# A two-layer gated cross-attention and expert model on one core: one pair's softmax sums moved from GpSimd's fold to ones products, and the first expert slots turned earlier

## What is computed

```python
x = x + tanh(g_xattn[0]) * L0_xattn(layernorm(x), ctx_1024, ...)    # 16 heads of 8
x = x + tanh(g_ffn[0])   * L0_ffn(layernorm(x), ...)                # 8 experts with low-rank parts, top 2
x = x + tanh(g_xattn[1]) * L1_xattn(ctx_1024, layernorm(x), ...)    # 16 heads of 64
x = x + tanh(g_ffn[1])   * L1_ffn(layernorm(x), ...)                # 8 experts, top 1
```

```python
dots = einsum('bhid,bhjd->bhij', q, k) * scale      # 256 queries, 768 keys (512 context, 256 latents)
attn = softmax(dots, axis=-1)
out  = einsum('bhij,bhjd->bhid', attn, v)           # then all heads @ Wout
```

## Time and profile before

| | |
|---|---|
| runs, us | 718.05 (717.65 to 720.27), n = 3 |
| profiled execution, us | 715.89 |
| its span, us | 714.1 |
| mean granted TensorE clock | 0.978 |
| TensorE, VectorE, ScalarE, GpSimd busy, us | 654.0, 526.4, 374.0, 354.2 |

### The profile page before, as it was taken

The page is one execution under the profiler, slowest core; times in us unless marked ns, Lnnn a source line. Parts: engine busy times, 40 slices in busy tenths (PEclk is TensorE's granted clock), DMA queues, the critical chain, the costliest instruction groups (busy, mean ns, idle before and its releaser), DMA issues.

```text
span 714.1 us, 14356 instructions
## 1 busy us (share of the span) xinstructions
PE 654.0 (92%) x5392; PEld 491.8 (69%) x5392; DVE 526.4 (74%) x1074; ACT 374.0 (52%) x581; POOL 354.2 (50%) x450
## 2 busy tenths in 40 slices
PE   5779999999989889899999999999999999779994
PEld 4656666666778777676777767777677776557884
DVE  5767887776598887798677777778889778746533
ACT  3656776665543444554464455545554446416652
POOL 3294444450034422566667566765666566680131
PEclk9779999999999999999999999999999999999997
DMA  8200000000300003000001000002000002010211
GB/s 187 25 0 2 2 2 3 2 2 1 120 3 1 0 1 111 2 1 1 2 1 31 16 2 16 17 14 61 1 3 1 1 2 60 21 51 12 67 49 56
DMA packets 35268, 16.97 MB, mean 24 GB/s; under 512 B 12824, under 2 KB 33648, under 8 KB 35072
## 3 DMA queue, kind: packets, MB, share of 16 engines
q1 hardware_dynamic: 33680, 14.94, 8.0%
q0 software_dynamic: 512, 1.05, 0.5%
q10 hardware_dynamic: 1008, 0.07, 0.1%
HBM read 12.05 MB, written 3.93 MB: 22 GB/s over the span
## 4 chain that ended last, share of the span: by engine, by line
PE 67%; DVE 20%; issue 6%; POOL 2%; ACT 1%; DMA 1%; SPq 0%; POOLq 0%; DVEq 0%; ACTq 0%
PE ps L1938 64%; DVE o L1638 3%; DVE pmax L1625 2%; PE ps L1949 2%; DVE mx L1308 2%; DVE kql L1613 1%; DVE exm L1504 1%; DVE pmax L1622 1%; POOL y_tok L726 1%; POOL xs_scratch L718 1%; PE ps L2042 1%; DMA raw<-in_L_xattn_Wproj_dram 1%; PE ps L2587 1%; DVE wsel L1501 0%; DVE rt_y L1415 0%
## 5 line engine op out<-in xcount | busy, mean ns | idle before, releaser
L1015 ACT ACTIVATE p<-ps 128x1024 f32<-128x1024 f32 x96 | 96.5, 1025 | 151.2 <-PE ps L1938 151.2
L752 POOL TENSOR_TENSOR acc<-p 128x256 f32<-128x256 f32 x128 | 94.9, 773 | 74.3 <-ACT p L1015 74.2
L1938 PE MATMUL ps<-p,v 128*64 128x256 f32 (+1 forms) x1280 | 123.4, 384 | 0.8 <-DVE xr L1334 0.6
L1938 PE MATMUL ps<-kqh 64*128 64x256 f32 (+1 forms) x640 | 111.3, 374 | 13.6 <-DVE pmax L1622 4.0
L758 POOL TENSOR_TENSOR acc<-acc,p 128x256 f32<-128x256 f32 x128 | 91.8, 749 | 54.2 <-ACT p L1015 54.1
L1622 DVE TENSOR_REDUCE pmax<-ps 128x2 f32<-128x1024 f32 x64 | 78.2, 1222 | 33.5 <-PE ps L1938 33.4
L1308 DVE TENSOR_REDUCE mx<-ps 128x1 bf16<-128x512 f32 x128 | 82.5, 687 | 26.6 <-PE ps L1938 26.0
L1938 PEld LDWEIGHTS ps<-p,v 128*64 128x64 f32 (+1 forms) x1280 | 66.1, 126 | 46.8 <-issue 15.3
L1938 PEld LDWEIGHTS ps<-kqh 64*128 64x128 f32 x640 | 62.6, 193 | 43.1 <-issue 34.4
L655 POOL TENSOR_SCALAR q<-qst,rmask 128x256 fp32r<-128x256 f32 x64 | 58.8, 939 | 59.2 <-ACT qst L775 59.2
L879 ACT ACTIVATE p<-ps 128x1024 f32<-128x1024 f32 x64 | 65.5, 1025 | 23.1 <-PE ps L1938 21.5
(11 more groups left out here) (318 smaller groups left out, 1431.5 us busy)
## 6 DMA issues: line engine op xcount, KB each, us to landing
w_raw<-in_L_ffn_W_dram SPq DMA_DIRECT2D x8, 256.0 KB, 2.7
ys_scratch<-y SPq DMA_DIRECT2D x22, 64.0 KB, 1.5
ctx_all<-in_ctx_dram SPq DMA_DIRECT2D x4, 256.0 KB, 5.6
raw_kv<-in_L_xattn_Wkv_dram SPq DMA_DIRECT2D x1, 1024.0 KB, 4.9
ctx_all<-in_L_ffn_W_dram SPq DMA_DIRECT2D x4, 256.0 KB, 3.6
w_raw_late<-in_L_ffn_W_dram SPq DMA_DIRECT2D x4, 256.0 KB, 3.8
xs_scratch<-xnA SPq DMA_DIRECT2D x1, 832.0 KB, 4.5
xs_rawA<-xs_scratch SPq DMA_DIRECT2D x3, 256.0 KB, 3.2
```

The costliest lines, as they stand in the source:

```text
L752: ins = pool.tensor_tensor(acc1[:, at], p1[:, s, 0, at], p1[:, s, 1, at], ALU.add)
L1015: act.activation(p1[:, g % 2, u, :], bank(2 * (n % 2), 2), ACT.Exp, scale=SCALE1).then_inc(a_exp1.sem, 1)
L1938: return pe.matmul(o, lhsT, rhs, start=start, stop=stop)
```

## The change

It makes three edits.

1. `UNFOLDED = G1 - 2 = 30`. GpSimd leaves out the adds and the fold of pair 30 (its scatters stay where they are), and the counts of g_acc and g_fold are made to fit. `sums1(30)` no longer waits for a fold: it multiplies each of the six chunks of p by the ones, both heads, 12 calls that accumulate into the same half of bank 6.
2. On TensorE `slots_turn(0)` is moved ahead of `outputs1_pairs(B - 1, range(NPAIR - 1))`.
3. On VectorE `slots_low(0)` is moved to between `w2_low(4)` and `w2_low(5)`; before it stood behind `w2_low(7)`.

```diff
--- before.py
+++ after.py
@@ -282,6 +282,7 @@
         TURN_SLOTS = (1, 5, 9, 11, 14, 18)
         EXP_SLOT = 4
         RANK_AT = (bank(7)[:, NQ:NQ + (TOKEN_TILES[0] + 1) * E], bank(7)[:, 0:(TOKEN_TILES[1] + 1) * E])
+        UNFOLDED = G1 - 2
         onecol = ident[:, MAXROW:MAXROW + 1]
         TURN_BANK = [4] + [7] * (B - 1)
         ROUTE_BANK = [5] + [7] * (B - 1)
@@ -744,20 +745,23 @@
                 s = g % 2
                 if g == G1 - 2:
                     scattered(0, xnA, range(TOKEN_TILES[0]))
+                if g == UNFOLDED:
+                    continue
+                n = g - int(g > UNFOLDED)
                 pool.wait_ge(a_exp1.sem, a_exp1.after(g, 2))
-                if g >= 1:
-                    pool.wait_ge(g_fold.sem, g)
+                if n >= 1:
+                    pool.wait_ge(g_fold.sem, n)
                 for c in range(4):
                     at = slice(c * NQ, (c + 1) * NQ)
                     ins = pool.tensor_tensor(acc1[:, at], p1[:, s, 0, at], p1[:, s, 1, at], ALU.add)
                 ins.then_inc(g_acc.sem, 1)
                 pool.wait_ge(a_exp1.sem, a_exp1.after(g, 3))
-                pool.wait_ge(g_acc.sem, g_acc.after(g, 1))
+                pool.wait_ge(g_acc.sem, g_acc.after(n, 1))
                 for c in range(4):
                     at = slice(c * NQ, (c + 1) * NQ)
                     ins = pool.tensor_tensor(acc1[:, at], acc1[:, at], p1[:, s, 2, at], ALU.add)
                 ins.then_inc(g_acc.sem, 1)
-                pool.wait_ge(g_acc.sem, g_acc.after(g, 2))
+                pool.wait_ge(g_acc.sem, g_acc.after(n, 2))
                 if g >= 2:
                     pool.wait_ge(e_den1.sem, g - 1)
                 a = acc1[:, :].rearrange("p (j n q) -> p j n q", j=2, n=2)
@@ -1114,7 +1118,7 @@
             def gelu(tile):
                 act.wait_ge(e_up.sem, tile + 1)
                 if tile == 0:
-                    act.wait_ge(g_acc.sem, g_acc.after(G1, 0))
+                    act.wait_ge(g_acc.sem, g_acc.after(G1 - 1, 0))
                 if tile >= 2:
                     act.wait_ge(e_hidT.sem, tile - 1)
                 act.activation(hid1[:, tile % 2, :], bank(UP_BANK[tile % 2]), ACT.Gelu).then_inc(a_gelu.sem, 1)
@@ -1766,7 +1770,7 @@
             def hidden_low(tile):
                 dve.wait_ge(a_hidH.sem, tile + 1)
                 if tile == 0:
-                    dve.wait_ge(g_acc.sem, g_acc.after(G1, 0))
+                    dve.wait_ge(g_acc.sem, g_acc.after(G1 - 1, 0))
                 if tile >= 2:
                     dve.wait_ge(e_down.sem, tile - 1)
                 dve.tensor_tensor(hidT_l[:, tile % 2, :], bank(HID_BANK[tile % 2]), hidT_h[:, tile % 2, :],
@@ -1894,9 +1898,11 @@
                 if g in W2_PAIRS:
                     w2_low(W2_PAIRS.index(g))
                 if g == G1 - 1:
-                    for e in range(2, E):
+                    for e in range(2, 5):
                         w2_low(e)
-            slots_low(0)
+                    slots_low(0)
+                    for e in range(5, E):
+                        w2_low(e)
             divide1(G1 - 1)
             for tile in range(SLOTS_ALL):
                 if tile == EXP_SLOT:
@@ -2448,9 +2454,16 @@
                 ins.then_inc(e_pv1.sem, 1)
 
             def sums1(g):
-                pe.wait_ge(g_fold.sem, g + 1)
-                for j in range(2):
-                    ins = mm(bank(6)[j * D1:(j + 1) * D1, NQ:2 * NQ], onesf[:, :], fold1[:, g % 2, j, :])
+                o = [bank(6)[j * D1:(j + 1) * D1, NQ:2 * NQ] for j in range(2)]
+                if g == UNFOLDED:
+                    for k in range(TK):
+                        for j in range(2):
+                            ins = mm(o[j], onesf[:, :], p1[:, g % 2, k // 2, j * BANK + (k % 2) * NQ:j * BANK + (k % 2 + 1) * NQ],
+                                     k == 0, k == TK - 1)
+                else:
+                    pe.wait_ge(g_fold.sem, g + int(g < UNFOLDED))
+                    for j in range(2):
+                        ins = mm(o[j], onesf[:, :], fold1[:, g % 2, j, :])
                 ins.then_inc(e_den1.sem, 1)
 
             def outputs1(b):
@@ -2657,8 +2670,8 @@
 
             expert = list(experts_in(0))
             pe.wait_ge(d_route.sem, d_route.after(0, 5))
+            slots_turn(0)
             outputs1_pairs(B - 1, range(NPAIR - 1))
-            slots_turn(0)
             sums1(G1 - 1)
             up1(0)
             for tile in range(SLOTS_ALL):
```

## The result

The changed kernel takes 712.28 us in the median of 12 runs (709.87 to 714.83). The kernel before is at 716.83 us in 12 runs (713.61 to 720.27), of which the prediction knew three, with a median of 718.05. The medians differ by 4.55 us. The ratio is 0.9934, 95% interval 0.9915 to 0.9952: by it 4.7 us less, between 3.4 and 6.1. The profiled execution takes 712.78 us with a span of 710.8, against 715.89 and 714.1: 3.3 us of span.

The account below looks back on a forecast made before the run. The seam's chain was taken to run through GpSimd's late fold of pair 30 and VectorE's reciprocal, leaving TensorE a 3.72 us hole. Gains of 2.2 and 1.4 us sum to 3.6: 718.05 - 3.6 = 714.4 us, range 712.4 to 716.5.

Parts of the forecast that it names:

- link 1: Pair 30's sums: 24 ones entries in 2.64 us replace GpSimd's adds and fold, freeing pair 31's p x v 2.2 us earlier.
- (C): Rival: pair 30's ones products cost double, 5.3 us, so gain 0.95 us, 717.1 us; chance 0.08.
- Links 2 to 4: Pair 31's scores, a 1.4 us TensorE gap at the upper clock, p x v from 632.97, slots_turn(0) at 635.71, xs_l wait gone.
- (B): Rival: the new TensorE gap of 1.4 us lowers the clock for 3.4 us; gain 1.9 us, 716.1 us; chance 0.10.
- Links 5 and 6: Pair 31's fold is ready before its sums need it, so no wait; up1(0) starts at 639.85 instead of 643.47.
- Link 7: Moved w2_low(5..7) delay pair 31's divide; last output products wait 0 to 1.1 us, 0.6 covered by VectorE's later chain.
- the last sum: Whole-kernel forecast: base 718.05 us, the median of the runs shown, less the 3.6 us seam gain, 714.4 us.
- rival (A): Low clock stretch from 621.49, ahead of pair 30's p x v, is absent; gain 5.2 us, 712.8 us; chance 0.22.

Follow-up runs that it names:

- e5: Changed kernel with the 12 ones products of pair 30 done twice: 715.20 us, ratio 0.9970.
- b1: Kernel before, no edit, traced again: 28.0 us from slot_u to up1(0).
- e1: Changed kernel with only the sums of pair 30 by ones products, slots_turn(0) and slots_low(0) back in their old places: 713.64 us, ratio 0.9953.
- e9: Changed kernel with pair 30's ones products ahead of its p x v (bank 7) and 14 small useless products in TensorE's idle piece: 710.03 us, ratio 0.9917.
- e3: Changed kernel with 14 small useless products in TensorE's idle piece ahead of pair 31's last maxima: 711.12 us, ratio 0.9918.
- b2: Kernel before, no edit, traced again: 29.3 us from slot_u to up1(0).
- e8: Kernel before with 54 small useless products in the hole ahead of pair 30's ones product: 715.99 us, ratio 1.0003.
- e10: Kernel before with 14 small useless products in the earlier idle piece and 84 in the hole: 715.28 us, ratio 0.9990.
- e0: Changed kernel as it stands, timed again: 712.39 us, ratio 0.9936.
- e7: Changed kernel with slots_low(0) back behind w2_low(7), slots_turn(0) still early: 713.37 us, ratio 0.9952.

## Why the forecast was right in its links and short in its size

**Removed wait (link 1): right.** 24 entries, 2.76 us for 2.64 + 0.17 forecast, no idleness before them, reciprocal at 630.87 for 630.70. The entries did not take 0.2 us each, so (C) is out: e5 shows 0.22 us for a whole product. The output products, with a weight of 128x128 and a moving slice of 128 columns, cost as much with half the columns: 28 entries in 3.23 us are 0.23 us for each of the 14. So the products with a 128x64 weight cost half of that for a column. The starts differ too: in the trace of the changed kernel two entries of the ones products start 0.006 us apart (628.064 and 628.070), the next two 0.21 us later (628.279 and 628.285), and each is recorded with 0.38 us, while in the trace of before the output entries start one by one, 0.11 us apart (638.138, 638.249, 638.361). What makes the entries go in pairs is not shown; no run changed the form of these products.

**Links 2 to 4: right.** Gap 1.16 us for 1.4, p x v at 633.14 for 632.97, slots_turn at 635.89 for 635.71. The granted clock stayed at 1.00 over the new gap (1.16 us in each) in all four traces of the changed kernel; (B) is out as far as they go.

**Links 5 and 6: right.** Fold not waited for, up1(0) at 640.18 for 639.85; from slot_u the gain is 27.4 - 24.0 = 3.4 us for 3.6. The moves alone are 1.0 to 1.2 us of it for my 1.4.

**Link 7: right, one sign missed.** 0.67 us of waiting for the divide, forecast 0 to 1.1, free up to 0.6. That is just over the 0.6 that I had named as a sign of being wrong, and the wait for xnB, which I said would stay, is gone. Both are the cover of link (7) at work: this wait takes the place of that one, and the part behind up1(0) is no longer than before.

**The step that failed** is the last sum: "the median of the runs shown lies 2.2 above the profiled run, and the same difference from it gives 718.05 - 3.6". It comes out 2.1 us over the 712.28 measured, and both of its terms are mis-sized.
- The base, 1.2 us. I took the median of three runs for the kernel's: 718.05, where twelve give 716.83. The three lie in the upper part of a spread of 713.6 to 720.3; that is chance, not a mechanism. With 716.83 my gain would have given 713.2, inside the range.
- The gain, 3.6 us for 4.55 by the medians. Between the two traces it is 3.4, so the links were priced right. What I had wrong is one trace's clock taken for the kernel's, on both sides of the change.
  - Before the change I took the 1.12 us of the four fold entries and one low stretch behind the hole as given. The trace that I had shows the cheapest of four: 27.4, 28.0, 28.7, 29.3 us, mean 28.4. The others cost up to 1.9 us more, and no case of mine had them.
  - After the change I kept the early low stretch and gave rival (A), without it, a chance of 0.22. It is absent in two of four traces (24.0 and 24.0 with it, 22.4 and 22.4 without, mean 23.2).

By the four traces on each side the seam gains 28.4 - 23.2 = 5.1 us, with a standard error of 0.6. Over the timed runs of the study the means are 716.6 us (100 runs of before) and 712.2 (23 of the changed kernel), 4.4 us with a standard error of 0.4. The two agree within their errors, and 4.4 is the better figure. Both errors went the same way; and my range ended at 712.4 with the centre of case (A) at 712.8, so it left a spread of 0.4 us below a case that turned out to be half of the traces.

**Open.** What decides which low stretches an execution gets is not shown. Nor was the part ahead of slot_u taken apart, 614.5 to 618.1 us. It goes together with the clock at the start: in the first 60 us the granted clock is 0.50 for 13.7 us in eight of the eighteen traces (0.89 in the mean) and for 17.1 in ten (0.86). Seven of the eight have slot_u at 614.5 to 615.1, and all of the ten have it at 615.8 or later. Three traces lie another 2 us later (b1, e1, e9) for a reason that wasn't looked for. The slowest runs of the changed kernel (714.6 to 714.9) have no trace; they may have e5's longer early stretch, 6.8 us, or those 2 us.

## What to carry to other kernels

The hole in TensorE's work cost its waiting and the clock behind it, and the second part differed from run to run (3.4 to 7.3 us at 0.50 in four traces of one kernel); before pricing such a hole's removal, trace several executions and take the mean, and don't take the median of three runs for the base when single runs spread by 6 us. And when a wait is removed, ask what it had been hiding: here the stretch at 0.50 ahead of the hole, free before, became 1.5 us of the path in two of four traces, and with fourteen products without use in an idle piece (0.95 us in e3) it was absent from all four traces taken.

## What the hardware showed that I had not expected

- TensorE's granted clock was 0.50 for 10.2 us in one piece (b2, 628.48 to 638.72), though it worked 7.0 of them. The clock fell 2.2 us into a hole of 5.2 us and came back only 7.3 us after its end, with 0.26 us of idleness in that time.
- 54 small products ahead of 2.07 us of idleness did not keep the clock up (e8, 0.50 from 632.10 to 635.51); with 84 ahead of 0.43 us it stayed at 1.00 (e10). Each is one trace.
- GpSimd's four adds took 2.78 us alone (first group of pair 31, before) and 4.10 (e0) to 4.55 (e1, e7) beside a run of VectorE's w2_low, a subtraction of two SBUF tensors; its four hot casts took 1.96 us behind the last w2_low (before) and 3.35 beside it (the changed kernel).
